# Where the twelve loads of the score operands are issued from, and step lists laid out anew

## The reference

```
xn = layernorm(x)
v = xn @ v_w + v_b                                  # 16 heads of 16
qm, km = xn @ qmod_w + qmod_b, xn @ kmod_w + kmod_b # a bias per query and per key
qc, kc = xn @ cq_w, xn @ ck_w                       # 16 heads of 8
scores = causal_kern[i - j] + qm[i] + km[j] + 0.15 * (qc . kc) / sqrt(8)
attn = softmax(where(j <= i, scores, -1e9));  ctx = attn @ v
h = ln(xn + ctx @ out_w + out_b);  s = ln(h + gelu(h @ ffn_w1 + b1) @ ffn_w2 + b2)
gate, up = q4(xn) @ q4(w_gate).T, q4(xn) @ q4(w_up).T
y = q4(silu(gate) * up) @ q4(w_down).T
out = x + s * silu(y)
```

## Time and profile before

| | |
|---|---|
| time, median of 3 runs | 1970.54 us (1969.98 to 1972.34) |
| the profiled execution's own time | 1971.34 us |
| its span, first to last instruction | 1969.5 us |
| busy: PE, DVE, POOL, ACT | 1841.2, 1598.7, 1102.8, 900.4 us |
| head, to the first cT of the loop | 248.5 us |
| loop, 14 passes | 1567.0 us |
| end | 154.0 us |

### The profile page before, as it was taken

How to read it: one execution, slowest core, us unless ns; L and a number is a source line. 1 busy time by engine, 2 the same in 40 slices (tenths; PEclk the granted TensorE clock), 3 DMA queues, 4 the chain that set the end, 5 groups by cost and what they waited for, 6 DMA issues and landing times.

```text
span 1969.5 us, 41524 instructions
## 1 busy us (share of the span) xinstructions
PE 1841.2 (93%) x12508; PEld 1309.0 (66%) x12508; DVE 1598.7 (81%) x5214; ACT 900.4 (46%) x1816; POOL 1102.8 (56%) x788
## 2 busy tenths in 40 slices
...
GB/s 138 174 93 89 63 75 117 73 88 69 105 64 82 88 73 106 73 95 73 85 64 99 89 73 106 62 95 83 76 74 73 116 73 88 70 106 67 40 65 22
DMA packets 129154, 165.44 MB, mean 84 GB/s; under 512 B 9821, under 2 KB 90718, under 8 KB 129028
## 3 DMA queue, kind: packets, MB, share of 16 engines
...
## 4 chain that ended last, share of the span: by engine, by line
PE 59%; DVE 20%; issue 14%; ACT 3%; DMA 1%; DVEq 1%; POOL 1%; SPq 1%; ACTq 0%; POOLq 0%
PE ps L738 11%; PE ps L729 11%; PE ps L679 8%; PE ps L696 4%; PE ps L579 4%; PE ps L602 3%; PE ps L636 3%; DVE nmax L994 3%; PE ps L711 3%; PE ps L589 3%; PE ps L652 2%; PE ps L632 2%; DVE ps L994 2%; DVE st L916 2%; DVE slot L1061 1%
## 5 line engine op out<-in xcount | busy, mean ns | idle before, releaser
L1132 POOL TENSOR_TENSOR Pr<-Pr,Tz 128x768 f32<-128x768 f32 (+2 forms) x384 | 477.9, 1273 | 243.7 <-ACT Pr L802 242.7
L994 DVE CUSTOM_DVE_ANT_0 ps<-ps,future 128x512 f32<-128x512 f32 (+3 forms) x1024 | 474.9, 517 | 52.7 <-issue 52.4
L802 ACT ACTIVATE Pr<-ps 128x384 f32<-128x384 f32 x512 | 243.0, 489 | 370.0 <-PE ps L636 367.1
L729 PE MATMUL ps<-catT,w 128*128 128x256 f32 x1024 | 237.3, 380 | 0.7 <-ACT catT L867 0.7
L602 PE MATMUL ps<-KS,QS 108*128 108x512 bf16 (+3 forms) x1024 | 217.2, 303 | 21.0 <-DVE nmax L994 14.7
L738 PE MATMUL ps<-w,gT 128*128 128x256 f32 x1024 | 233.0, 381 | 0.9 <-ACT gT L878 0.9
L791 ACT ACTIVATE ps<-ps 128x512 f32<-128x512 f32 x256 | 150.5, 588 | 132.4 <-PE ps L632 130.2
L1024 DVE SCALAR_TENSOR_TENSOR Pr<-ps,Tz 128x512 f32<-128x512 f32 x256 | 175.0, 684 | 41.3 <-ACT ps L791 37.9
L738 PEld LDWEIGHTS ps<-w,gT 128*128 128x128 f32 x1024 | 190.9, 190 | 25.8 <-ACT gT L878 1.3
L729 PEld LDWEIGHTS ps<-catT,w 128*128 128x128 f32 x1024 | 189.7, 190 | 26.7 <-ACT catT L867 1.0
L696 PE MATMUL ps<-wdT,hqT 128*128 128x256 f32 x768 | 178.2, 381 | 0.7 <-ACT hqT L843 0.7
...
## 6 DMA issues: line engine op xcount, KB each, us to landing
Tz<-kernel_rows SPq DMA_DIRECT2D x128, 512.0 KB, 3.8
...
```

What stands on the lines that cost most here:

```text
L729: ins = mm(dst[:, i * n:(i + 1) * n], w1[:, c, f * P:(f + 1) * P], catT[:, c, hf * n:(hf + 1) * n], start=c == 0, stop=c == KD - 1)
L802: inc(af(Pr[:, p % 4, e, at:at + wd], src[:, 0:wd], ACT.Exp), "a_exp")
L994: ins = v.tensor_tensor_reduce(o, o, future[:, S - n:S], -1.0, 3e38, ALU.add, ALU.min, nmax[:, 2 * pl + e, it:it + 1])
L1132: ins = g.tensor_tensor(a, a, Tz[:, p % 2, :, P * j:P * j + PAST[j]], ALU.mult)
```

## The change

The step load moves from the sync engine's code to ScalarE's, with the same waits and the same six DMAs (in the head one wait more, for the first splitio's earlier count). The lists of all engines and parts are laid out anew. In the loop the sync engine's and ScalarE's read:

```diff
         sync="""
-            T.0 load.1 T.1 T.2 xload T.3 mio.1 T.4 splitio T.5 load.0 T.6 T.7 fin mio.0
+            T.0 T.1 T.2 xload T.3 mio.1 T.4 splitio T.5 T.6 T.7 fin mio.0
         """,
         scalar="""
-            cT sc.0.0 vcopy silu.0.0 sc.0.1 silu.0.1 sc.0.2 sc.0.3 sc.0.4 sc.0.5 sc.1.0 hT silu.1.0 sc.1.1 sc.1.2
+            cT sc.0.0 load.1 silu.0.0 vcopy sc.0.1 silu.0.1 sc.0.2 sc.0.3 sc.0.4 sc.0.5 sc.1.0 silu.1.0 hT sc.1.1
...
-                elif k == "load":
-                    half = s[1]
-                    hb = half_batch(half, b)
-                    if which != "pro":
-
-                        E["pe_sc"].wait(sp, hb - 1, 24 * half + 23)
...
-                    d_split.wait(sp, hb)
...
-                    for dst, src in loads:
-                        sp.dma_start(dst, src).then_inc(d_load[half].sem, 16)
...
+                elif k == "load":
+                    half = s[1]
+                    hb = half_batch(half, b)
+                    if which != "pro":
+
+                        E["pe_sc"].wait(act, hb - 1, 24 * half + 23)
...
+                    d_split.wait(act, hb)
...
+                    for dst, src in moves:
+                        act.dma_start(dst, src).then_inc(d_load[half].sem, 16)
```

More of the change, by code:

```diff
@@ L90 @@
         vector="""
[L91 to L100, removed]
@@ new lines @@
+            pro:projm.0 pre:sin.5 pre:sin.6 pro:projm.1 pro:projm.2 pro:load.0 pro:load.1 pre:sin.7 pre:sin.8
+            pre:sin.9 pre:sin.10 pre:peak pre:sin.11 pre:sin.12 pre:sin.13 pre:sin.14 pre:sin.15 pre:tanh pro:mT.0
+            pre:wt.0 pre:wt.1 pre:wt.2 first:xT.0 pre:wt.3 pre:wt.4 first:xT.1 pre:wt.5 pre:wt.6 first:vcopy pre:wt.7
+            first:proj.0 first:proj.1 pre:dexp pre:wt.8 first:proj.2 pro:xqT first:silu.0.0 first:projm.0 first:sc.0.0
+            first:silu.0.1 first:sc.0.1 first:silu.1.0 first:sc.0.2 first:sc.0.3 first:sc.0.4 first:sc.0.5
@@ L168 @@
         """,
         vector="""
-            out.0 out.1 ln1 muld.0.0 silu.0.0 lnc1 silu.0.1 muld.0.1 mx.1.0.0 lnb1 mx.1.0.1 mx.1.0.2 muld.1.0 mx.1.0.3
-            silu.1.0 mx.1.0.4 mx.1.1.0 muld.1.1 mx.1.1.1 mx.1.1.2 mx.1.1.3 mx.1.1.4 muld.2.0 mx.1.2.0 mx.1.2.1 hq.0
-            mx.1.2.2 mx.1.2.3 norm mx.1.2.4 mx.1.3.0 muld.2.1 mx.1.3.1 mx.1.3.2 mx.1.3.3 mx.1.3.4 muld.3.0 mfin.1 hr.0
-            silu.1.1 f2.0 muld.3.1 proj.0 hq.1 f2.1 ctxt.0 proj.1 proj.2 muld.4.0 hr.1 xq muld.4.1 xr xr2 silu.2.0
@@ L174 @@
-            muld.5.0 silu.2.1 hq.2 v.0 v.1 muld.5.1 f2.2 hr.2 mx.0.0.0 mx.0.0.1 f2.3 ln2 mx.0.0.2 mx.0.0.3 muld.6.0
-            silu.3.0 ctxt.1 muld.6.1 lnc2 lnb2 mx.0.0.4 mx.0.1.0 dn.0 silu.3.1 muld.7.0 mx.0.1.1 mx.0.1.2 mx.0.1.3
-            mx.0.1.4 hq.3 muld.7.1 mx.0.2.0 mx.0.2.1 mx.0.2.2 mx.0.2.3 mx.0.2.4 dn.1 ctxt.2 hr.3 mx.0.3.0 mx.0.3.1
-            dn.2 mx.0.3.2 mx.0.3.3 mx.0.3.4 mfin.0 ctxt.3 dn.3
+            out.0 out.1 ln1 muld.0.0 silu.0.0 lnc1 silu.0.1 muld.0.1 lnb1 mx.1.0.0 mx.1.0.1 muld.1.0 mx.1.0.2 mx.1.0.3
@@ L211 @@
         vector="""
-            last:silu.0.0 last:out.0 last:muld.0.0 last:out.1 last:ln1 last:silu.0.1 last:lnc1 last:mx.1.0.0
-            last:mx.1.0.1 last:muld.0.1 last:lnb1 last:silu.1.0 last:muld.1.0 last:mx.1.0.2 last:hq.0 last:mx.1.0.3
-            last:mx.1.0.4 last:hr.0 last:muld.1.1 last:mx.1.1.0 last:mx.1.1.1 last:silu.1.1 last:mx.1.1.2
-            last:mx.1.1.3 last:mx.1.1.4 last:mx.1.2.0 last:mx.1.2.1 last:mx.1.2.2 last:hq.1 last:muld.2.0
-            last:mx.1.2.3 last:hr.1 last:mx.1.2.4 last:mx.1.3.0 last:f2.0 last:muld.2.1 last:f2.1 last:mx.1.3.1
@@ L217 @@
-            last:mx.1.3.2 last:mx.1.3.3 last:mx.1.3.4 last:mfin.1 last:muld.3.0 last:muld.3.1 last:silu.2.0
-            last:silu.2.1 last:muld.4.0 last:hq.2 last:muld.4.1 last:ctxt.0 last:hr.2 last:muld.5.0 last:f2.2
-            last:dn.0 last:silu.3.0 last:muld.5.1 last:silu.3.1 last:muld.6.0 last:hq.3 last:f2.3 last:muld.6.1
-            last:ln2 last:muld.7.0 last:muld.7.1 last:dn.1 last:dn.2 last:ctxt.1 last:lnc2 last:lnb2 last:ctxt.2
-            last:ctxt.3 last:hr.3 tail:out.0 tail:out.1 tail:ln1 tail:lnc1 tail:lnb1 last:dn.3 tail:f2.0 tail:f2.1
```

263 lines of the change are left out of this document (142 added, 121 removed).

## The result

The changed kernel takes 1977.43 us (median of 9 runs, 1975.89 to 1979.53) against 1970.54 for the kernel before (9 runs beside them, 1967.21 to 1974.41). The ratio is 1.0032, 95% interval 1.0022 to 1.0042. Faster was forecast.

The account below looks back on a forecast made before the run. PE, busy 108.58 of 112 us a loop period, was taken as the bound, paced at the loop's top by DVE's lnb1. 1971.34 - 7 (loop) - 1.5 (head) = 1962.8, so 1962.0 us for the median; range 1950 to 1985.

Parts of the forecast that it names:

- Price of the issues, 2.75 us for six: Loop, load.1 on ScalarE: six issues take 2.75 us, the tanh is 0.4 us later, DVE's chain 0.15 us.
- an issue of 0.8 us or more: Sign of being wrong: issues on ScalarE this long, where 0.3 to 0.5 us each was expected.
- Load.0 covered, splitio 3 to 4 us sooner: Loop: splitio lands sooner, so load.0 on ScalarE costs nothing; if splitio stays put, 1.5 to 2 us a period.
- Load.1 meets PE, price 0: Top of the loop: load.1 lands at 821.6, PE reaches mx.1.0.0 at 821.7; cost 0, upper end 2.2 us.
- hT 0.5 us sooner, 0.5 us a period: Loop: lnb1 right behind muld.0.1 starts hT sooner, winning 7 us in 14 passes; bounds 0 to 0.8 a period.
- nothing comes of it: Rival for the loop: later waits eat the hT gain, leaving the head's 1.5 us; 1969 us, chance 0.22.
- Head: 1.5 us won, between 4 lost and 6 won: Head: statistics and copies moved ahead of proj.0 fill about 3.5 of DVE's 9.33 idle us; later soft gives back 1.5 to 3.
- the 251: Sign of being wrong: a loop entry later than 251 us; it was 248.47 in the kernel before.
- the slow rival: Loop: loads on ScalarE come late and the kernel is slower, 1976 to 1985 or 1990 to 2003 us; chance 0.28.
- End: 0 within 2: End, 154 us: a serial tail behind the last pv with its loads covered; change 0, within 2 us either way.

Follow-up runs that it names:

- loadone: The kernel before with only the loop's load.1 moved from the sync engine to ScalarE, behind the exp of sc.0.0: 1989.39 us, ratio 1.0091.
- queueback: The changed kernel with its new lists, but the twelve loads issued by the sync engine again: 1972.71 us, ratio 1.0011.
- projfirst: The kernel before with all loads on ScalarE and, in the loop, proj.1 and proj.2 (DVE), projm.1 and projm.2 (POOL) moved up: 1997.04 us, ratio 1.0144.
- headload: The changed kernel with only the head's load.0 of batch 0 moved back to the sync engine: 1977.82 us, ratio 1.0031.
- firstold: The changed kernel with batch 0's steps in the head in the order of before, in the same slots: 1977.97 us, ratio 1.0033.

## Why the prediction was wrong, step by step

- **Price of the issues, 2.75 us for six**: 2.34 in the undisturbed case, and the tanh is 0.19 us late where 0.4 was said (0.15 for DVE's chain). That holds for the tanh ahead of vcopy; with vcopy between them, in loadone, DVE's chain is 0.9 late. But one issue sometimes takes longer. In the pass from 703.00 of the changed kernel:

```profile
709.42 0.93 ACTq L769 DMA_DIRECT2D KS<-k_bias_parts  x1
...
712.07 0.46 ACT L832 ACTIVATE th<-ps 128x352 f32<-128x352 f32 x1 [2.56 <-PE ps L614]
```

  0.93 in place of 0.47, and that pass is 112.14 long, not 111.70. ScalarE stands ahead of hT's chain, so each such issue of load.1 is paid nearly in full; the prediction had named an issue of 0.8 us or more as a sign of being wrong. This makes the loop's gain 2.2 us in one profile and 1.0 in the other. queueback has no such pass.
- **Load.0 covered, splitio 3 to 4 us sooner**: right (3.6 us sooner; no wait of ScalarE). projfirst shows what an earlier splitio is worth in the old lists, 6.1 us a pass, more than the 1.5 to 2 that the prediction set for the case without it.
- **Load.1 meets PE, price 0**: right in sign; PE doesn't wait. The landing was estimated at 7.5 us from the first issue. loadone shows 6.6, against 9.8 in the earlier trace rows, where T.1 went out right behind it. By the Trainium skill (DMA: Bandwidth & Descriptors, Issuing engines are not separate DMA queues) another issuing engine brings no DMA engines of its own; no run here shows a load that is faster by its queue with the same traffic beside it.
- **hT 0.5 us sooner, 0.5 us a period**: the first half was right (0.62), the second failed, and it was the largest term of the sum (7 us). A pass gained 0.23, and 0.16 of that is the place in mfin.0, which no step of the prediction had. lnb1's 1.67 us on DVE moved in front of the maxima, and PE paid there: its wait for the maxima grew from 3.6 to 10.1 us in the 14 passes, 0.46 a pass. The rival "nothing comes of it" had named this. I asked what waits for lnb1, and not who waits for what lnb1 now pushes back.
- **Head: 1.5 us won, between 4 lost and 6 won**: this step turned the sign. The head lost 7.4 us, and the entry at 255.86 is past the 251 that the prediction had named as a sign of being wrong. It worked out the prologue up to soft and left batch 0 of the head, behind the first muld, at nothing without a reason. The first muld came 0.8 us sooner; behind it the new lists lose 8.2 us (76.1 to 84.3; 7.4 in the second profile): 2.4 to 3.2 by load.0 on ScalarE ahead of the exp of sc.3.5, shown by headload and queueback, and about 5 by the order, of which it is shown where they arise and not why. The mechanism of the slow rival, a load on ScalarE that blocks an exp, was right, but I had looked for it in the loop alone, where the lists cover it.
- **End: 0 within 2**: 3.0 and 1.2 us in two profiles, within what the end varies by in kernels with either list. Of the 3.0, 0.5 arise in the tail's cT and 2.4 in the out rows behind it, both at the lower clock.

What stays open: which steps make the 5 us of batch 0's order and how much of it is the clock (0.88 of 84.3 us in the changed kernel, so 10 us of full-speed time missing; 0.94 of 81.1 in queueback and headload, 5 us; 1.00 before); why the second step of mfin.0 follows the first after 0.23 us behind the new prologue and 0.40 behind the old one, in the same loop; and why firstold's and headload's medians don't show what their stretches do.
